# Twelve broadcast loads for sixteen in the sixteen-head layer's stacks, and its first maxima a step earlier

## The reference, cut to what matters

```python
def _L1_attn_ref(x, w_qkv, w_out):                      # B 2, S 1024, E 128, H 16, D 8
    q, k, v = ((x @ w_qkv).reshape(b, s, 3, H, D).transpose(2, 0, 3, 1, 4))
    scores = einsum('bhsd,bhtd->bhst', q, k) / sqrt(D)
    attn = softmax(scores)
    return einsum('bhst,bhtd->bhsd', attn, v) ... @ w_out
x = x + _L0_attn_ref(norm(x)); x = x + _L0_ffn_ref(norm(x))
x = x + _L1_attn_ref(norm(x)); x = x + _L1_ffn_ref(norm(x))
```

## Time and profile before

| what | value |
|---|---|
| median of 3 runs | 1060.2 us (1058.15 to 1062.98) |
| the profiled execution's own time | 1063.73 us |
| its span | 1061.9 us, 18838 instructions |
| mean granted TensorE clock | 0.963 |
| TensorE matmul busy | 975.9 us (92%) |
| VectorE busy | 808.6 us (76%) |
| ScalarE busy | 705.1 us (66%) |
| GpSimd busy | 277.1 us (26%) |

### The profile page before, as it was taken

How to read it: one execution, slowest core, us unless ns; L and a number is a source line. 1 busy time by engine, 2 the same in 40 slices (tenths; PEclk the granted TensorE clock), 3 DMA queues, 4 the chain that set the end, 5 groups by cost and what they waited for, 6 DMA issues and landing times. The chain is left out here.

```text
span 1061.9 us, 18838 instructions
## 1 busy us (share of the span) xinstructions
PE 975.9 (92%) x6760; PEld 537.2 (51%) x6760; DVE 808.6 (76%) x1369; ACT 705.1 (66%) x1355; POOL 277.1 (26%) x288
## 2 busy tenths in 40 slices
PE   5499998899999999789889999999999899999997
PEld 3256686466666666442123222222222477888885
DVE  8968656467755855577878999999994478777877
ACT  6323458555544675324787888888887797888885
POOL 1137532526545545123212200000100013112201
PEclk9599999899999999888989999999999999999999
DMA  5000005796955856503001100000200103311111
GB/s 107 1 2 2 31 8 222 224 298 199 238 153 167 241 150 164 127 19 109 17 16 46 60 17 16 21 26 17 22 1 2 41 1 133 108 60 60 40 40 40
DMA packets 56580, 86.16 MB, mean 81 GB/s; under 512 B 15136, under 2 KB 33192, under 8 KB 55464
## 3 DMA queue, kind: packets, MB, share of 16 engines
q1 hardware_dynamic: 52088, 78.66, 25.2%
q0 software_dynamic: 3968, 6.10, 2.6%
q10 hardware_dynamic: 432, 0.20, 0.1%
HBM read 63.76 MB, written 21.43 MB: 80 GB/s over the span
## 5 line engine op out<-in xcount | busy, mean ns | idle before, releaser
L2421 ACT ACTIVATE narrow_att_probs<-psum 128x512 f32<-128x512 f32 x512 | 264.7, 604 | 73.6 <-PE psum L2341 73.2
L2468 DVE TENSOR_REDUCE front_maxima<-psum 128x1 f32<-128x1024 f32 x240 | 282.1, 1219 | 23.7 <-PE psum L1190 19.1
L2341 PE MATMUL psum<-narrow_att_q,narrow_att_k 50*128 50x512 bf16 x448 | 146.2, 384 | 5.6 <-ACT narrow_att_probs L2421 4.7
L1190 PE MATMUL psum<-narrow_att_k,narrow_att_q 48*128 48x512 bf16 x448 | 133.4, 386 | 13.3 <-DVE front_maxima L2468 5.4
L2354 PE MATMUL psum<-narrow_att_probs,narrow_att_v_ones 128*32 128x512 f32 x1024 | 138.8, 615 | 0.1
L2951 DVE TENSOR_TENSOR moe_hidden_lo<-moe_hidden,moe_hidden_hi 128x512 fp32r<-128x512 f32 x144 | 104.4, 751 | 38.9 <-ACT moe_hidden_hi L2853 38.3
L2849 ACT ACTIVATE moe_hidden<-psum,back_up_bias 128x512 f32<-128x512 f32 x144 | 96.3, 690 | 32.8 <-PE psum L73 32.8
L2039 DVE TENSOR_REDUCE gated_nmax<-psum 128x1 f32<-128x1024 f32 x62 | 73.0, 1220 | 50.4 <-PE psum L1709 50.1
L1784 ACT ACTIVATE lead_room<-psum 128x512 f32<-128x512 f32 x62 | 33.8, 595 | 101.8 <-PE psum L1658 101.7
L1190 PEld LDWEIGHTS psum<-narrow_att_k,narrow_att_q 48*128 48x128 bf16 x448 | 25.7, 95 | 148.5 <-DVE front_maxima L2468 131.2
L1561 POOL DMA_INDIRECT home_rows<-gated_y,gated_to_row x62 | 62.0, 1000 | 133.2 <-ACT gated_y L1779 123.5
(11 more groups left out here) (458 smaller groups left out, 1876.5 us busy)
## 6 DMA issues: line engine op xcount, KB each, us to landing
gated_k_ring<-gated_k_dram SPq DMA_DIRECT2D x62, 288.0 KB, 4.7
lead_room<-gated_v_dram SPq DMA_DIRECT2D x32, 256.0 KB
moe_mixb<-moe_mix_scratch SPq DMA_DIRECT2D x8, 1024.0 KB, 4.8
gated_k_dram<-gated_keys SPq DMA_DIRECT2D x8, 512.0 KB, 5.7
gated_v_dram<-gated_v_stage SPq DMA_DIRECT2D x2, 2048.0 KB, 8.4
lead_wqk_hi<-gated_v_dram SPq DMA_DIRECT2D x16, 256.0 KB
lead_wqk_lo<-gated_v_dram SPq DMA_DIRECT2D x14, 256.0 KB
gated_q_dram<-lead_room SPq DMA_DIRECT2D x8, 256.0 KB, 2.3
```

What stands on the lines that cost most here:

```text
L1190: return pe.matmul(out, self.stack(0, n // 2)[64 * a:64 * a + self.ROWS, n % 2, r, tile(qt)], self.stack(1, n // 2)[64 * a:64 * a + self.R ...
L2341: pe.matmul(psum[:, SCORE_BANK + j % 3, :], ks(n // 2, kt // QT, e)[rows, tile(kt % QT)], qs(n // 2, n % 2, e)[rows, :], start=True, stop= ...
L2421: act.activation(probs[:, k % 3, 2 * e + u % 2, :], psum[:, SCORE_BANK + j % 3, :], ACT.Exp, scale=SCALE).then_inc(exped, 1)
L2468: dve.tensor_reduce(maxima[:, n % 2, at:at + 1], chunk.rearrange("p a b -> p (a b)"), AX.X, ALU.max).then_inc(chunk_used, 1)
```

## The change

- The slots of a stack are filled in another order: q as q0 q1 q2 q0 q1 q0, k as k0 k0 k0 k1 k1 k2. The six products are the same six, added in another order. Each slot table has three entries now. For q: parts 0 to 2 into slots 0 to 2 (24 partitions), parts 0 and 1 into slots 3 and 4 (16), part 0 into slot 5 (8). For k: part 0 three times (24), part 1 twice (16), part 2 once (8). So 6 loads for a stack, 12 for a group; the bytes are the same.
- The remainder of `fproj` 3 gets its middle part at the end of step 24 on ScalarE, behind that step's jobs, and its low part on GpSimd right behind the other three. SyncE stores all twelve pieces, waits for them and issues the loads of group 0 behind the loads of p = 26.
- The maxima start in step 26: four in each of steps 26 to 30, ten in step 31, two in step 32.

```diff
-    Q_SLOTS = ((0, 2, 3), (1, 1, 1), (1, 5, 1), (2, 0, 1))
-    K_SLOTS = ((0, 0, 3), (1, 3, 1), (1, 5, 1), (2, 4, 1))
-    LOADS = 2 * 2 * 4
+    Q_SLOTS = ((slice(0, 3), 0, 1), (slice(0, 2), 3, 1), (slice(0, 1), 5, 1))
+    K_SLOTS = ((slice(0, 1), 0, 3), (slice(1, 2), 3, 2), (slice(2, 3), 5, 1))
+    LOADS = 2 * (3 + 3)
...
-        for s, first, n in (self.Q_SLOTS, self.K_SLOTS)[m]:
+        for parts, first, times in (self.Q_SLOTS, self.K_SLOTS)[m]:
             for a in range(2):
...
-                src = self.parts_dram[m, s, g // self.PERG].rearrange("(a d g) h r t -> a g d (h r t)", a=2, d=self.DH)[a, g % self.PERG]
+                src = self.parts_dram[m, parts, g // self.PERG].rearrange("s (a d g) h r t -> a g s d (h r t)", a=2, d=self.DH)[a, g % self.PERG]
+                row, n = 64 * a + first * self.DH, src.shape[0] * times * self.DH
+                if times > 1:
+                    src = src[0].unsqueeze(0).to_broadcast([times, self.DH, 2 * self.PAIRS * BANK])
...
-                25: [("fvalue", 1)], 27: next_maxima[0:4], 28: next_maxima[4:8], 29: next_maxima[8:12], 30: next_maxima[12:16],
-                31: next_maxima[16:30], 32: next_maxima[30:] + [("nshift",)]}
+                25: [("fvalue", 1)], 26: next_maxima[0:4], 27: next_maxima[4:8], 28: next_maxima[8:12], 29: next_maxima[12:16],
+                30: next_maxima[16:20], 31: next_maxima[20:30], 32: next_maxima[30:] + [("nshift",)]}
...
-        MIDDLE_AT = {24: (0, 1, 2), 25: (3,)}
+        MIDDLE_AT, LAST_MIDDLE = {24: (0, 1, 2)}, (24, 3)
...
                 if p == 26:
-                    for k in (0, 1, 2):
+                    for k in range(2 * PERB):
                         front.store_parts(sp, k, front_part)
-                if p == 27:
-                    front.store_parts(sp, 3, front_part)
                     sp.wait_ge(front.parts_stored[0], front.PARTS_B)
                     for m in range(2):
                         front.load_stack(sp, 0, m)
...
+                if p + 2 == LAST_MIDDLE[0]:
+                    front.lowest(pool, LAST_MIDDLE[1], front_part, front_rest)
...
+                if j == LAST_MIDDLE[0]:
+                    front.middle(act, LAST_MIDDLE[1], front_part, front_rest)
```

More of the change, by code:

```diff
@@ L1160, in load_stack @@
         stack = self.stack(m, g)
-        for s, first, n in (self.Q_SLOTS, self.K_SLOTS)[m]:
+        for parts, first, times in (self.Q_SLOTS, self.K_SLOTS)[m]:
             for a in range(2):
-                row = 64 * a + first * self.DH
-                src = self.parts_dram[m, s, g // self.PERG].rearrange("(a d g) h r t -> a g d (h r t)", a=2, d=self.DH)[a, g % self.PERG]
-                eng.dma_start(stack[row:row + n * self.DH].rearrange("p h r t -> p (h r t)"),
-                              src.unsqueeze(0).to_broadcast([n, self.DH, 2 * self.PAIRS * BANK])).then_inc(self.stacked[g], 16)
+                src = self.parts_dram[m, parts, g // self.PERG].rearrange("s (a d g) h r t -> a g s d (h r t)", a=2, d=self.DH)[a, g % self.PERG]
+                row, n = 64 * a + first * self.DH, src.shape[0] * times * self.DH
+                if times > 1:
+                    src = src[0].unsqueeze(0).to_broadcast([times, self.DH, 2 * self.PAIRS * BANK])
+                eng.dma_start(stack[row:row + n].rearrange("p h r t -> p (h r t)"), src).then_inc(self.stacked[g], 16)
     def load_ones(self, sp, dst, loaded):
```

## The result

The changed kernel takes 1069.95 us (median of 5 runs, 1067.38 to 1071.95) against 1059.84 for the kernel before (5 runs on the same chip, 1057.46 to 1062.98): ratio 1.0096 [1.0068, 1.0124], 10.1 us slower. Forecast were 1063.6 us and a range to 1067.5. The direction was right; the size is three times the forecast and lies outside the range. The profiled executions differ by less, 1069.7 - 1061.9 = 7.8 us of span: the one of before lay 3.9 us above its median (1063.73), the one after 1.6 us above (1071.54).

A forecast was written before the change was run, and what follows sets the result against it. Bound: TensorE busy 92% of 1061.9 us, a ring of waits across engines at 395 to 520 us. +3.1 from the late stack and +0.3 at half 5 make +3.4 on 1060.2: 1063.6 us, range 1057.5 to 1067.5.

The forecast's parts named there:

- The formula: Time change from T, when the first maxima (`nmax`) product runs: T after minus 429.99 plus 5.97; T 427.1 gives +3.1 us.
- First load at 412.3: SyncE's first group 0 stack load, after stores landing in 3.0 us: 412.3 (411.4 to 413.8), 5.5 us earlier.
- Two engines for a two-block copy, six issues as long as eight: Stack loads: 16-partition copies run on two engines, 6.4 us a stack against 4.5; issue 3.7 us, no gain.
- Loads take 14.8 us: Group 0, first load issue to first maxima product: 14.8 us, against 12.2 before.
- 12.0 of transfer: Both group 0 stacks back to back on the busiest engine: 1.04 + 67 x 0.163 = 12.0 us.
- 1.4 to the first row: Group 0 loads: 1.4 us from issue to first row, taken from an undisturbed stack.
- The 1.4 left for landing, wake and disturbance: Group 0, last load term before the product: 1.4 us, bounds 0.7 and 2.5.
- The bound of 16 us: Worst case for group 0, load issue to product: 16 us, with the disturbance term at 2.5.
- even loads: Rival: group 0 load time goes with copy number, 9.2 us; T 421.5, -2.5 us, 1057.7; chance 0.14.
- loads as long as before: Rival: group 0 loads still take 12.2 us; T 424.5, +0.5 us, 1060.7; chance 0.2.
- Slow stores: Rival: stores before group 0's loads land after 4.5 us, disturbance 2.5; T 429.7, +5.7 us, 1065.9; chance 0.16.
- Half 5: Shift issued at 604.16 behind a q stack lands near 609, first score at 608.81: 0.3 us (0 to 1.5).

The follow-up runs named there:

- slots_alone: Kernel before with only the new slot tables and twelve loads; schedule, stores and maxima as before: 1090.25 us, ratio 1.005 to the kernel before.
- ring_held: Changed kernel with SyncE waiting until both group 0 stacks have landed before issuing the next value and key loads: 1089.0 us, 1.0054 to the kernel before.
- after_again: Changed kernel unaltered, run once more on a chip like the first: 1069.73 us, ratio 1.0097 to the kernel before.
- gathers_early: Changed kernel with GpSimd's gathers of the last three pairs issued at pair 21: 1066.57 us, ratio 1.0067 to the kernel before.
- sooner_gathers: Kernel before with early split and stores, its sixteen loads at pair 26, last three pairs' gathers at pair 21, old maxima order: 1058.42 us, 0.9986.
- single_slots: Kernel before with early split and stores, loads at pair 26 as 24 single 8-partition copies, old maxima order: 1057.84 us, 0.9986.
- ring_first_new_slots: Kernel before with early split, stores and gathers, the change's twelve loads issued behind pair 27's values and pair 28's keys, old maxima order: 1094.31 us, 1.0082.

## Why the prediction was wrong in size

- **The formula** (T after - 429.99 + 5.97) held for the profile, not quite for the time. With the score of step 26 as zero it gives 23.89 - 20.92 + 5.97 = +8.9 us, and the offset of the two traces grows by 8.7 from there to the issue of the first shift behind the maxima (485.51 after, 475.77 before, less the 1.04). It gives slots_alone (+5.9 for +5.7) and ring_held (+4.7 for +4.5) well, after_again and gathers_early less (+7.9 for +9.6, +4.0 for +6.4). So 1.2 us of the change's loss by one profile, 1.7 by the other, have no place in it. For sooner_gathers and single_slots it would give -6.6 and -5.9 for -1.7 and -2.3: it assumes that nothing but the stack stands between T and the tail, and there step 28 stood.
- **First load at 412.3**: measured 413.88 - 1.04 = 412.8, and 413.5 in after_again by the same clock. SyncE waits 3.5 and 4.2 us for the stores, above the 3.0 taken and within the bounds. gathers_early (1.6 us) shows what lengthens this wait.
- **Two engines for a two-block copy, six issues as long as eight**: right, 6.3 us a stack for 6.4, 3.55 to 4.01 us of issue for 3.7. A 16-partition copy, for which there was no row, takes about 0.6 us to issue (0.7 was taken).
- **"Loads take 14.8 us"** is the step that failed: 20.1 in the profile, 18.4 in the second. Of its terms, 12.0 of transfer became 15.2 (13.9 in the second), and 1.4 to the first row became 3.2 (2.9). The 1.4 left for landing, wake and disturbance was spent on the landing alone (1.7 and 1.6). The transfer term was taken from an undisturbed stack. A check on the kernel before would have warned: the same working gives its two stacks, with 44 rows on the busiest engine, 1.04 + 43 x 0.163 = 8.0 us, and from first to last row they took 9.4. The text had seen that `load_v(27)` and `load_k(28)` move behind the stack loads, but asked only whether their users would wait, not what their bytes do to two engines that are the bound. ring_held shows it: without them 11.7 us of transfer, and a loss of 4.5 us for the changed kernel's 10 (its and the change's intervals overlap, and the chips differ; the transfer is the firmer reading). The first-row term was also taken undisturbed; gathers_early shows 1.6 us without gathers. In slots_alone the first row comes after 1.6 us as well, with the same two-block copies, so it is not they that delay it. The bound of 16 us held all disturbance in one term of 2.5, taken from loads that had three and eight engines to go to.
- **The parts against the whole**: by their medians +5.7 us for the slots and +0.6 for the order make 6.3, against 9.6 and 10.1 for both. That is no proof of something between them: the intervals of the parts reach 4.0 us to either side for the slots and 2.8 for the order, the chips differ, and by the stretch they make 5.9 + 1.4 = 7.3 for 7.9 and 8.9. More traffic on the whole is not the reason either: the rows take 15.0 us in slots_alone, where later values and keys lie beside them too, for 13.9 and 15.2.
- **Rivals**: even loads and loads as long as before are excluded by slots_alone. Slow stores came nearest in size (+5.7), by the wrong mechanism: it wanted a landing 1.5 us later than forecast, and the stores gave 0.5 and 1.2 of that; the loads gave 5.3 and 3.6.
- **Half 5**: 0.28 us more there (offset of issues 7.49 before it, 7.77 after), forecast 0.3. Some 2.2 us of the offset are given back before that, in the first halves of the third layer: 9.74 at the first shift, 8.80 at the second, 7.65 at the third, 7.50 at the fourth. A part falls where TensorE's clock was low before (0.50 of full) and was not after (1.00 over 515.7 to 539.1); that the clock is the cause is not shown. The stretch before:
```profile
509.00:511.00 2.00, 2.00 (x12) 0.48 (x8) 1.03 (x2) 0.95 (x3) 1.92 (x3) 0.50 0.14 17
```

The Trainium skill's rule ("DMA: Bandwidth & Descriptors", section "Why a DMA increments its semaphore by 16 and not by 1") is that a copy runs on the largest number of engines up to 16 that divides the slowest dimension of both its sides; for a copy of two blocks that is two. This trace agrees: 0.12 of sixteen engines at the end of an undisturbed stack, and two chains of rows at the end of group 0's.

## What to carry to other kernels

Count the engines that a copy is spread on, not the copies: here twelve loads in blocks of two and three were slower than sixteen (8 us, ring_first_new_slots) and than 24 of one block each (10 us). A transfer bound by two engines is also open to whatever the other traffic puts on these two, so its time from a quiet stretch is a lower end (12.0 us against 13.9 to 15.2 here). And when issues are moved ahead in one queue, everything moved behind them is to be asked twice: who waits for it, and whom its bytes meet.

## What was not expected of the hardware

A 4 KB row takes 0.16 us on an engine in a quiet stretch and 0.36 on average, over 2 us of group 0's stacks, when all sixteen are busy. With gathers lying on the engines a stack's first row came 1.3 to 1.6 us later, and the landing of the stores before it 2.6 us later. One chip runs the same kernel 2.3% slower than the others (1084.5 to 1085.0 for 1059.8 to 1060.2), with stands of 1 to 8 us, releaser remote in the trace, that the others do not show; differences of 5 us read on one chip should not be set against those of another.
